# Rotary attention: the row maxima run two heads ahead of the exponentials in place of three

## The reference, cut to what matters

```python
x = x + _L1_attn_ref(_layernorm(x), w_qkv, w_out, b_out)      # x: 4 sequences of 1024 tokens, 128 wide

q, k, v = split(x @ w_qkv); each cut into H = 16 heads of 8
q = q * cos + rotate_half(q) * sin;  k likewise
dots = einsum('bhid,bhjd->bhij', q, k) * 8 ** -0.5
attn = softmax(dots, axis=-1)
out  = einsum('bhij,bhjd->bhid', attn, v)
return out.transpose(...).reshape(b, n, 128) @ w_out + b_out
```

## Time and profile before

| | us |
|---|---|
| median of 3 runs (2882.84, 2884.83, 2890.88) | 2884.83 |
| the profiled execution, its own time | 2889.47 |
| its span | 2887.7 |
| first `big` matmul of the stage (start) | 991.8 |
| first `small` matmul of the stage (start) | 1021.7 |
| last evacuation of a head's sums (start) | 1763.24 |

### The profile page before, as it was taken

How to read it: one execution, slowest core, us unless ns; L and a number is a source line. 1 busy time by engine, 2 the same in 40 slices (tenths; PEclk the granted TensorE clock), 3 DMA queues, 4 the chain that set the end, 5 groups by cost and what they waited for, 6 DMA issues and landing times. The chain is left out here.

```text
span 2887.7 us, 45476 instructions
## 1 busy us (share of the span) xinstructions
PE 2290.7 (79%) x13880; PEld 1435.5 (50%) x13880; DVE 2041.1 (71%) x5186; ACT 1454.3 (50%) x3123; POOL 925.2 (32%) x978
## 2 busy tenths in 40 slices
PE   3399598849967699999999897758958597788887
PEld 3389477749944222222222223448947597523334
DVE  4466688856644699999999981555658565679994
ACT  2266311116633478888888885216633365533332
POOL 5644235544433301010110000463426544223330
PEclk9999799969988789999999998879979699889998
DMA  4122200002220400000000000012221123100001
GB/s 156 46 60 62 62 8 16 16 27 60 65 79 10 165 16 19 19 17 21 18 18 19 17 7 31 23 36 60 66 70 34 47 64 90 48 0 0 1 0 30
DMA packets 111195, 115.76 MB, mean 40 GB/s; under 512 B 21904, under 2 KB 94192, under 8 KB 110192
## 3 DMA queue, kind: packets, MB, share of 16 engines
q1 hardware_dynamic: 92512, 76.38, 9.0%
q0 software_dynamic: 17408, 35.95, 3.7%
q10 hardware_dynamic: 1040, 0.53, 0.1%
HBM read 67.55 MB, written 44.83 MB: 39 GB/s over the span
## 5 line engine op out<-in xcount | busy, mean ns | idle before, releaser
L1882 DVE TENSOR_REDUCE attn_mx<-bank 128x1 f32<-128x512 f32 x1024 | 641.3, 683 | 61.1 <-PE bank L1661 52.9
L1783 ACT ACTIVATE attn_pT<-bank 128x512 f32<-128x512 f32 x1024 | 540.0, 603 | 125.4 <-PE bank L1676 124.9
L1661 PE MATMUL bank<-attn_K,attn_Q 48*128 48x512 bf16 x1024 | 336.3, 396 | 50.9 <-DVE attn_mx L1882 29.2
L1676 PE MATMUL bank<-attn_Q,attn_K 51*128 51x512 bf16 x1024 | 330.7, 386 | 2.4 <-ACT attn_pT L1783 1.6
L1689 PE MATMUL bank<-attn_pT,attn_vb 128*32 128x512 f32 x2048 | 275.7, 610 | 20.1 <-ACT attn_pT L1783 12.1
L1842 POOL TENSOR_TENSOR attn_m_rem<-attn_m_rem,attn_m_parts 8x128 f32<-8x128 f32 x128 | 53.5, 418 | 678.1 <-ACT attn_m_parts L1796 678.1
L1661 PEld LDWEIGHTS bank<-attn_K,attn_Q 48*128 48x128 bf16 x1024 | 71.8, 94 | 375.3 <-DVE attn_mx L1882 323.2
L2638 POOL TENSOR_TENSOR mix_rS<-mix_rT,mix_S 128x512 f32<-128x512 f32 x64 | 80.2, 1254 | 185.3 <-DVE mix_S L2697 91.9
L1004 PE MATMUL bank<-mix_prod_qk,ident 128*128 128x256 f32 x512 | 118.7, 386 | 0.0
L1004 PEld LDWEIGHTS bank<-mix_prod_qk,ident 128*128 128x128 f32 x512 | 99.7, 195 | 28.4 <-issue 16.0
L828 POOL DMA_INDIRECT y_rows<-ffn0a_ys,ffn0a_to_row x72 | 69.2, 961 | 96.0 <-DVE ffn0a_ys L859 95.4
(11 more groups left out here) (617 smaller groups left out, 5882.8 us busy)
## 6 DMA issues: line engine op xcount, KB each, us to landing
w<-in_L_w SPq DMA_DIRECT2D x4, 2048.0 KB
ffn0a_x_ring<-xs_rows SPq DMA_DIRECT2D x72, 65.0 KB, 1.8
ffn0b_x_ring<-xs_rows SPq DMA_DIRECT2D x72, 65.0 KB
ffn2a_x_ring<-xs_rows SPq DMA_DIRECT2D x72, 65.0 KB, 1.8
ffn2b_x_ring<-xs_rows SPq DMA_DIRECT2D x72, 65.0 KB, 1.8
ffn0a_y_back<-y_rows SPq DMA_DIRECT2D x8, 512.0 KB, 3.9
ffn1a_in_y_back<-y_rows SPq DMA_DIRECT2D x8, 512.0 KB
ffn2a_y_back<-y_rows SPq DMA_DIRECT2D x8, 512.0 KB
```

Source lines behind the costliest of these rows:

```text
L1661: nc.tensor.matmul(a_bank[n % 3][:], slot(net.Q, h, 0, KROWS)[:, qt * P:(qt + 1) * P], slot(net.K, h, 0, KROWS)[:, hf * CH:(hf + 1) * CH], ...
L1676: nc.tensor.matmul(s_bank[n % 3][:], slot(net.K, h, 0, KROWS + MROWS)[:, kt * P:(kt + 1) * P], slot(net.Q, h, 0, KROWS + MROWS)[:, hf * CH ...
L1783: nc.scalar.activation(pT[:, kt % RING, hf * CH:(hf + 1) * CH], s_bank[(n * HPB + hf) % 3][:], ACT.Exp, scale=HD ** -0.5).then_inc(exp_rea ...
L1882: nc.vector.tensor_reduce(mx[:, h % 2, qt, hf:hf + 1], a_bank[n % 3][:], AX.X, ALU.max).then_inc(a_used, 1)
```

## The change

One constant, read in four places: the number of prologue heads of PE (L1743) and of DVE (L1923), and the head whose `big` and `largest` ride in pass h (L1750 and L1927).

```diff
 QRING = 4
 HRING = 2 * QRING
-LEAD = 3
+LEAD = 2
 MROWS = 3
 VCOL = 32
```

## The result

The changed kernel takes 3139.69 us (median of 4 runs, 3102.83 to 3215.59) against 2884.40 us (4 runs, 2882.84 to 2890.88), 255 us or 8.9% more. The ratio of the means, 1.0838 with a 95% interval of 1.0739 to 1.0936, leaves out the longest run, which counts as a slow one. I had forecast 2875.1 us and a range up to 2882. The runs of the changed kernel also lie far apart, 113 us where those of before span 8.

A forecast was written before the change was run, and what follows sets the result against it. The prediction took the cycle of `small`, `exp` and `pv` to set a pass, and DVE's reductions the prologue. It summed -9.85 + 0.08 = -9.77 us, other terms 0, so 2884.83 became 2875.06 us; range 2869 to 2882.

The forecast's parts named there:

- One prologue head less: Prologue: sixteen `big`, sixteen reductions and one `nm` reduction go from before the first `small`; -9.85 us.
- One pass with `big` in place of one without: Pass 61: the removed head's work reappears there, so the pass costs 11.23 in place of 11.15 us; +0.08 us.
- Rings and queues: Loop: `nm` entries free as early as before, loads gain a pass of slack, engines keep their issue order; cost 0.
- Cover of head 0's rows: Behind the prologue: the DMAs of head 0's maxima land before the first `small`, margin 3.8 us; cost 0.
- The `turn`: PE's transpose of `nm` in each pass: slack shrinks by one head but 1.19 us of margin stays; 0 us.
- The rival on the slower side: Loop: the `turn` waits for DVE's `nm` in every pass; with 0.5 us each, +21 us, 2906 us; chance 0.04.
- My sign of being wrong: Mid-stage: if passes are longer than 11.23 us, the step about the `turn` fails.
- PE's clock: First `small` and sequence ends: low-clock penalty unchanged in the mean, 2.9 us either way at the start, 3 at the ends.
- The forecast of -9.8 us: Whole kernel: the shorter prologue less the dearer pass, -9.77 us from the median, 2875.06 us; chance 0.80.

The follow-up runs named there:

- lead2_other_half: The changed kernel (LEAD = 2) with slots dealt out so that heads h and h + 2 lie in different partition halves; 2879.56 us against 2887.53, ratio 0.9975.
- lead3_pairs_in_order: The kernel before (LEAD = 3) with both `big` of a tile issued ahead of both `small`; 2923.48 us (one run).

## Why the prediction was wrong

- **One prologue head less: right.** From the first `nm` to the first `small` it was 1021.66 - 1002.10 = 19.56 us; in the changed kernel it is 1013.51 - 1003.34 = 10.17, so 9.39 us less for the 9.85 forecast. In lead2_other_half it is 1006.62 - 996.83 = 9.79, 9.77 less. The first `small` of the changed kernel stands behind a `big` on its own half, which explains the difference: one start at 1.2 GHz is 0.43 us.
- **One pass with `big` in place of one without: the step that failed.** I priced a pass with `big` at 11.23 us and the exchange at +0.08, because "nearly all of the maxima work is hidden". That holds as long as `big` runs beside `small`. I read "hidden" as beside DVE and ACT, and did not ask how PE found the time or whether the change keeps it. In all the passes with `big`, not only in the one that I counted, the head beside `small` is now another, and the head decides the partition half. No term of the sum asked for this; it went in at nothing without a reason. The runs showed 12.76 - 11.23 = 1.53 us in each of 62 passes at full clock, 94.9 us, and lead2_other_half showed that it goes away when only the halves are changed.
- **Rings and queues: incomplete.** I wrote that the engines issue `over`, `gather`, the evacuation and the work at a sequence's end "in the same order between the same neighbours. Cost 0." This is true of those. It passes over `big` and `small`, whose order is the same but whose heads are not.
- **Cover of head 0's rows: right.** The DMAs were issued from 1006.10, and no wait for them stands ahead of the first `small`. The 2.0 us of the Trainium skill ("DMA: Bandwidth & Descriptors", the anatomy of one DMA) are given there for DMAs issued from GpSimd, and these are issued from SP; the term did not rest on it.
- **The `turn`: right.** Its weight load goes on with idle time put down to "issue" (0.43 us at 1226.62 and in the passes beside it), and in lead2_other_half the same lead runs at 11.23 us a pass. The rival on the slower side had the right sign by the wrong mechanism. My sign of being wrong, that longer passes would mean a failed `turn`, pointed at the wrong step.
- **PE's clock: failed as a consequence.** I took it as unchanged within 2.9 us. Over 1012 to 2093 the mean granted clock was 0.75, that is half of 1081 us, 540 us, at 1.2 GHz. At 22.95 us a pass these are 23.5 passes, each 10.19 us dearer than at full clock: 240 us.

The sum for the profiled executions: 94.9 + 240 - 9.4 = 325 us. From the first `nm` to the last evacuation the stage took 1088.70 us in place of 761.14, 327.6 more, and the spans differ by 3213.8 - 2887.7 = 326.1 us. For the median, 3139.69 - 2884.40 = 255.3 us, the first and the third term are the same and about 170 us are left for the low clock. That split is worked out, not read from a trace, but the granted clocks of the four runs bear it out. Over the whole launch these were 0.842, 0.862, 0.865 and 0.875 in the mean, for 3215.59, 3146.61, 3132.76 and 3102.83 us: the less of the low clock, the shorter the run. Why the clock falls at one pass and not at another I could not settle: in the profiled execution it fell in pass 8, came back in pass 9 and then held through passes 10 to 17. In this stage long stretches at 1.2 GHz, 30 us and more behind the prologue, appear only in the kernels in which `big` and `small` share a half in every pass (and, with `small` on 128 rows, not even there). Shorter falls also occur where they overlap, as at the sequence ends of the kernel before.

The rows for it were in the trace before. The PE timeline mid-stage shows `big` and `small` starting within 0.01 us of each other, and `slot` says in one line on what that rests. The forecast of -9.8 us was sound for the prologue. Of it 8.0 us are left in the medians of lead2_other_half (-0.25%, interval -0.42 to -0.08%) and 7.75 in its trace, from the first `nm` to the last evacuation (753.39 us in place of 761.14); about 2 us come back behind the first `small`. That is the size that I had allowed for the clock, but no run shows that the clock is the cause.

## What to carry to other kernels

When a loop runs one head's work beside another's, ask not only how far apart they are but which slot each falls into: here the parity of the lead decided whether two matmuls ran at once. Before calling PE work hidden, look at the starts of neighbouring matmuls; if two start together, find out what lets them and whether the change keeps it. The lead and the slot layout are one decision, to be changed together.

## What the runs showed of the hardware

- Two bf16 matmuls over 48 and 51 partitions start within 0.01 us of each other when one stands on partitions 0 to 63 and the other on 64 to 127; on one half they start 0.22 us apart at 2.4 GHz and 0.43 us apart at 1.2 GHz. A matmul on the free half started ahead of one issued before it (1142.62 against 1142.84, lead3_pairs_in_order).
- PE busy for 200.00 of 200.00 us (1200 to 1400) was granted 0.50 with `small` on 51, 64 or 96 partitions and `big` on 48 of the same, and 1.00 with `small` on 128.
- With `small` on 128 or 96 partitions and `big` on 48 of the same, the weight load no longer ran beside a matmul: starts 0.32 us apart at 2.4 GHz in place of 0.22 (128 partitions), and 0.54 us apart at 1.2 GHz in place of 0.43 (96).
